# Two elementwise products moved to GpSimd, and the LayerNorm centring moved into PSUM

## The chip, the cores and the metric

The kernel runs on the 8 cores of one Trainium2 chip. Every core does the same program on one of 8 sequences, and nothing passes between cores. The metric is device time in microseconds (us) of the slowest core. The kernel before takes 775.81 us, the median of 3 runs (775.62 to 777.02).

## The reference

Per sequence, x is [2048, 1024]. A LayerNorm of x feeds two branches: a linear attention in chunks of 128 tokens with 16 heads of 64 and a decay per head, and a dense layer g with a SiLU.

```python
q, k, v = silu(x @ Wq), silu(x @ Wk), silu(x @ Wv)
def step(kv, (qi, ki, vi)):                  # per head, chunk of 128 tokens
    scores = (qi @ ki.T) * mask
    o = scores @ vi + lam_q[:, None] * (qi @ kv)
    kv = lam_c * kv + (ki * lam_k[:, None]).T @ vi
    return kv, o
o = (o - mean(o)) * rsqrt(var(o) + EPS) * gamma + beta    # over all 1024 features
gate = sigmoid(x @ Wg1 @ Wg2)
y = x0 + ((o * gate) @ Wo) * silu(x @ (W + lilora).T + b)
```

## The kernel before, in words

The script lists the operations of each engine in program order. A helper (`_emit`) turns the tiles that an operation reads and writes into semaphore waits. An engine does its own list strictly in order, so an instruction that waits holds back all that is listed behind it. A `Buf` stands for a tile or a part of one: `bPB[i]` for PSUM bank i (128 partitions of 512 f32), `bQH[0..1]` and `bKV[0..1]` for the two halves of QH and KVBD.

Five stages follow one another: LayerNorm of x, with q and k; v; the attention loop over 16 chunks (lines 592 to 706); the weights of the second branch, the gate and g; and a last stage of 16 token tiles.

The attention loop, for chunk c. TensorE computes the scores of 16 heads into banks 1 to 4 (L599, L605) and transposes K (L626, bank 0). VectorE multiplies the scores by the mask (L613, L619, twice each, into SAB), K by its decay (L631, KTM) and Q by its decay (L638, QH). Then come two halves w = 0, 1 of four head pairs: TensorE does V times scores (L649), adds the product of the carried state KVBD and QH (L662, not in chunk 0), both into banks 6 and 7, and the new state term (L669, bank 5). VectorE scales the old state half (L675) and adds bank 5 to it (L696, L701). ScalarE copies banks 6 and 7 over VO (L685, L691), the tile that L649 and L669 have read, so it waits for L669. The transposed output O thus takes the place of V. L675 of the second half is listed behind the additions of the first half and has to wait for them, since both write the same `bKV` half.

The last stage is ordered A(0), B(0), then A(tc), S(tc-1), B(tc) for tc = 1 to 15, then S(15). `p4c_A` computes the mean: eight matmuls against a column of ones (L881), a copy with 1/E (L886, MROW), an f32 matmul that spreads the row over 128 partitions (L889); VectorE subtracts it from O (L892, CC), ScalarE squares CC (L898). `p4c_B` sums the squares (L909), takes the root (L914, VROW), spreads it (L918), inverts it (L921, RBI), and does two operations on each of eight 128-column pieces of CC: times gamma and RBI (L926), plus beta and times the gate (L932). `p4c_S` multiplies piece by piece of CC with the weights, two matmuls of 512 columns for each (L946), into banks 4 and 5 for even tiles and 6 and 7 for odd ones; VectorE multiplies by G (L953) and a DMA on GpSimd's queue adds the tile to y in HBM (L958). CC has two copies, for even and odd tiles.

GpSimd has otherwise casts of small weights and one large copy of x to y, issued ahead of the attention loop (L588).

Of the kernel before, what the change touches and what calls it, by code (L numbers as in the profile page):

```python
# [8 lines left out]
AF = mybir.ActivationFunctionType  # L9
ALU = mybir.AluOpType  # L10

T = 2048
E = 1024
# [169 lines left out]
def build(debug_taps=(), stage=4):  # L183
# [82 lines left out]
    VO = mk("VO", [128, 16384], BF16, offset=off["VO"])  # L266
# [325 lines left out]
    for c in range(NCH):  # L592
# [32 lines left out]
        for f in range(8):  # L625
# [9 lines left out]
        qsrc = A(QT, 0, c * 128, [[2048, 8], [1, 128]])  # L635
        qdst = A(QH, 0, csl * 1024, [[128, 8], [1, 128]])
        lsrc = A(LAMQB, 0, 0, [[128, 8], [1, 128]])
        p.dve(lambda e, qsrc=qsrc, qdst=qdst, lsrc=lsrc: e.tensor_tensor(  # L638
            out=qdst, in0=qsrc, in1=lsrc, op=ALU.mult),
            reads=[bQT[pp][c // 4] for pp in range(8)] + [bLAMQ],  # L640
            writes=[bQH[csl]])
# [1 line left out]
        for w in range(2):  # L643
            sa, sb = 1 + 2 * w, 2 + 2 * w
            for i in range(4):
                pp = w * 4 + i
                ob = 6 + i // 2
                ocol = (i % 2) * 256
                p.pe(lambda e, pp=pp, c=c, ob=ob, ocol=ocol, w=w, i=i: e.matmul(  # L649
                    PB[ob][:, ocol:ocol + 256],  # L650
                    VO[:, c * 1024 + pp * 128:c * 1024 + (pp + 1) * 128],
                    A(SAB, 0, w * 1024 + i * 256, [[1, 256]]),
                    start=((i % 2) == 0), stop=(c == 0 and (i % 2) == 1)),
                    reads=[bVO[c][w], bSAB[w]], writes=[bPB[ob]])
            if c > 0:
                for i in range(4):
                    pp = w * 4 + i
                    ob = 6 + i // 2
                    ocol = (i % 2) * 256
                    rhs = bass.AP(QH, csl * 1024 + pp * 128,  # L660
                                  [[2048, 128], [0, 2], [1, 128]])
                    p.pe(lambda e, pp=pp, ob=ob, ocol=ocol, rhs=rhs, csl=csl, i=i: e.matmul(  # L662
                        PB[ob][:, ocol:ocol + 256],
                        KVBD[:, csl * 1024 + pp * 128:csl * 1024 + (pp + 1) * 128],
                        rhs, start=False, stop=((i % 2) == 1)),
                        reads=[bKV[csl], bQH[csl]], writes=[bPB[ob]])
            for i in range(4):
                pp = w * 4 + i
                p.pe(lambda e, pp=pp, c=c, csl=csl, i=i: e.matmul(  # L669
                    PB[5][:, i * 128:(i + 1) * 128],  # L670
                    KTM[:, csl * 1024 + pp * 128:csl * 1024 + (pp + 1) * 128],
                    VO[:, c * 1024 + pp * 128:c * 1024 + (pp + 1) * 128],
                    start=(i == 0), stop=(i == 3)),
                    reads=[bKTM[csl], bVO[c][w]], writes=[bPB[5]])
            p.dve(lambda e, csl=csl, nsl=nsl, w=w: e.tensor_tensor(  # L675
                out=KVBD[:, nsl * 1024 + w * 512:nsl * 1024 + (w + 1) * 512],
                in0=KVBD[:, csl * 1024 + w * 512:csl * 1024 + (w + 1) * 512],
                in1=LAMCB[:, w * 512:(w + 1) * 512], op=ALU.mult),
                reads=[bKV[csl], bLAMC], writes=[bKV[nsl]])
            for bb_ in range(2):  # L680
                ob = 6 + bb_
                dstA = A(VO, 0, c * 1024 + (w * 4 + bb_ * 2) * 128,
                         [[128, 2], [1, 128]], rowcount=64)
                srcA = A(PB[ob], 0, 0, [[256, 2], [1, 128]], rowcount=64)
                p.act(lambda e, d=dstA, s=srcA: e.activation(  # L685
                    out=d, in_=s, func=AF.Copy),
                    reads=[bPB[ob]], writes=[bVO[c][w]])
                dstB = A(VO, 64, c * 1024 + (w * 4 + bb_ * 2) * 128,
                         [[128, 2], [1, 128]])
                srcB = A(PB[ob], 64, 128, [[256, 2], [1, 128]])  # L690
                p.act(lambda e, d=dstB, s=srcB: e.activation(  # L691
                    out=d, in_=s, func=AF.Copy),
                    reads=[bPB[ob]], writes=[bVO[c][w]])
            oA = A(KVBD, 0, nsl * 1024 + w * 512, [[128, 4], [1, 64]], rowcount=64)
            iA = A(PB[5], 0, 0, [[128, 4], [1, 64]], rowcount=64)
            p.dve(lambda e, oA=oA, iA=iA: e.tensor_tensor(  # L696
                out=oA, in0=oA, in1=iA, op=ALU.add),
                reads=[bPB[5], bKV[nsl]], writes=[bKV[nsl]])
            oB = A(KVBD, 64, nsl * 1024 + w * 512 + 64, [[128, 4], [1, 64]])
            iB = A(PB[5], 64, 64, [[128, 4], [1, 64]])  # L700
            p.dve(lambda e, oB=oB, iB=iB: e.tensor_tensor(  # L701
                out=oB, in0=oB, in1=iB, op=ALU.add),
                reads=[bPB[5], bKV[nsl]], writes=[bKV[nsl]])
# [170 lines left out]
    def p4c_A(tc):  # L874
        par = tc % 2
        sb_st = [0, 2][par]
        sb_b = [1, 3][par]
        CCt, C2t = CCs[par], C2s[par]
        bCCt, bC2t = bCCs[par], bC2s[par]
        for pp in range(8):  # L880
            p.pe(lambda e, tc=tc, pp=pp, sb_st=sb_st: e.matmul(  # L881
                PB[sb_st][0:1, 0:128], ONESB[:, 0:1],
                VO[:, tc * 1024 + pp * 128:tc * 1024 + (pp + 1) * 128],
                start=(pp == 0), stop=(pp == 7)),
                reads=[bONESB, bVO[tc][pp // 4]], writes=[bPB[sb_st]])
        p.act(lambda e, sb_st=sb_st: e.activation(  # L886
            out=MROW[:], in_=PB[sb_st][0:1, 0:128], func=AF.Copy, scale=1.0 / E),
            reads=[bPB[sb_st]], writes=[bROW])
        p.pe(lambda e, sb_b=sb_b: e.matmul(  # L889
            PB[sb_b][:, 0:128], ONESF[:], MROW[:], start=True, stop=True),  # L890
            reads=[bONESF, bROW], writes=[bPB[sb_b]])
        p.dve(lambda e, tc=tc, CCt=CCt, sb_b=sb_b: e.tensor_tensor(  # L892
            out=A(CCt, 0, 0, [[128, 8], [1, 128]]),
            in0=A(VO, 0, tc * 1024, [[128, 8], [1, 128]]),
            in1=A(PB[sb_b], 0, 0, [[0, 8], [1, 128]]),
            op=ALU.subtract),
            reads=bVO[tc] + [bPB[sb_b]], writes=[bCCt] + bCCP[par])
        p.act(lambda e, CCt=CCt, C2t=C2t: e.activation(  # L898
            out=C2t[:], in_=CCt[:], func=AF.Square),
            reads=[bCCt] + bCCP[par], writes=[bC2t])  # L900

    def p4c_B(tc):
        par = tc % 2
        sb_st = [0, 2][par]
        sb_b = [1, 3][par]
        CCt, C2t = CCs[par], C2s[par]
        bCCt, bC2t = bCCs[par], bC2s[par]
        for pp in range(8):
            p.pe(lambda e, pp=pp, C2t=C2t, sb_st=sb_st: e.matmul(  # L909
                PB[sb_st][0:1, 128:256], ONESB[:, 0:1],  # L910
                C2t[:, pp * 128:(pp + 1) * 128],
                start=(pp == 0), stop=(pp == 7)),
                reads=[bONESB, bC2t], writes=[bPB[sb_st]])
        p.act(lambda e, sb_st=sb_st: e.activation(  # L914
            out=VROW[:], in_=PB[sb_st][0:1, 128:256],
            func=AF.Sqrt, scale=1.0 / E, bias=EPS),
            reads=[bPB[sb_st], bEPS], writes=[bROW])
        p.pe(lambda e, sb_b=sb_b: e.matmul(  # L918
            PB[sb_b][:, 128:256], ONESF[:], VROW[:], start=True, stop=True),
            reads=[bONESF, bROW], writes=[bPB[sb_b]])  # L920
        p.dve(lambda e, sb_b=sb_b: e.reciprocal(  # L921
            out=RBI[:], in_=PB[sb_b][:, 128:256]),
            reads=[bPB[sb_b]], writes=[bB128])
        for pp in range(8):
            bP = bCCP[par][pp]
            p.dve(lambda e, CCt=CCt, pp=pp: e.scalar_tensor_tensor(  # L926
                out=CCt[:, pp * 128:(pp + 1) * 128],
                in0=CCt[:, pp * 128:(pp + 1) * 128],
                scalar=GAMB[:, pp * 128:pp * 128 + 1],
                in1=RBI[:], op0=ALU.mult, op1=ALU.mult),  # L930
                reads=[bP, bB128, bLAMC], writes=[bP])
            p.dve(lambda e, tc=tc, CCt=CCt, pp=pp: e.scalar_tensor_tensor(  # L932
                out=CCt[:, pp * 128:(pp + 1) * 128],
                in0=CCt[:, pp * 128:(pp + 1) * 128],
                scalar=BETB[:, pp * 128:pp * 128 + 1],
                in1=GATE[:, pp * 2048 + tc * 128:pp * 2048 + (tc + 1) * 128],
                op0=ALU.add, op1=ALU.mult),
                reads=[bP, bBETB, bGATE[pp][tc // 4]], writes=[bP])
# [85 lines left out]
```

How the kernel before makes its waits and increments, by code:

```python
                def _run(eng):  # L119
                    for fn, waits, sem, step in self.ops[stream]:
                        for (sn, sv) in waits:
                            eng.wait_ge(self.sems[sn][0], sv)
                        if fn is not None:
                            ins = fn(eng)
                            if step:
                                ins.then_inc(self.sems[sem][0], step)
```

## Time and profile before

| | |
|---|---|
| median of 3 runs | 775.81 us |
| the profiled execution, its own time | 774.9 us |
| its span on the slowest core (core 5) | 773.3 us |
| spans of the 8 cores | 766.5 to 773.3 us |
| TensorE matmul busy | 522.2 us, 68% |
| VectorE busy | 320.6 us, 41% |
| ScalarE busy | 226.8 us, 29% |
| GpSimd busy | 19.5 us, 3% |

A busy share is an average over stages that have different limits, so the stage and its chain of waits have to be read, not the share. In the profile PE is TensorE, DVE is VectorE, ACT is ScalarE, POOL is GpSimd. PEclk is TensorE's granted clock: 1.0 is 2.4 GHz and 0.5 is 1.2 GHz, and a value between is a stretch with both. Bars of matmuls are modelled and overlap; starts are the safer thing to compare.

### The profile page before, as it was taken

How to read it: one execution, taken by the hardware profiler on the slowest of the kernel's cores; microseconds unless marked ns; L12 is line 12 of the kernel's file. 1: busy time of each engine (PE TensorE's matmuls, PEld its weight loads, DVE VectorE, ACT ScalarE, POOL GpSimd, SP SyncE). 2: the span in 40 equal slices, each digit the busy share in tenths (PEclk: the TensorE clock that was granted, in tenths of full speed). 3: DMA queues.
4: the chain of work that ended last, by engine and by line, in shares of the span. 5: the costliest groups of instructions: out<-in, count | busy, mean ns of one | idle time of the engine just before them, and what ended most of it. 6: DMA issues, size and time to landing. Idle time of an engine off the chain costs nothing.

```text
span 773.3 us, 8400 instructions; the slowest of 8 cores (766.5 to 773.3 us)
## 1 busy us (share of the span) xinstructions
PE 522.2 (68%) x2678; PEld 248.2 (32%) x2678; DVE 320.6 (41%) x675; ACT 226.8 (29%) x425; POOL 19.5 (3%) x28
## 2 busy tenths in 40 slices
PE   0118273999999971566556565799995776777673
PEld 0003131444444430344334343124442232323221
DVE  1350605110120004665566654610005777777784
ACT  1134443566333320223222232373332011111110
POOL 0000000000000000000000001000000000000000
PEclk9999595999999995555655666559997778677877
DMA  8671302000159983000000001150000332233233
GB/s 247 213 256 34 112 24 83 0 1 1 65 167 181 174 182 125 0 1 1 1 0 2 1 1 38 55 163 1 1 0 1 55 55 41 42 56 54 32 51 56
DMA packets 14049, 49.73 MB, mean 64 GB/s; under 512 B 3728, under 2 KB 3729, under 8 KB 13878
## 3 DMA queue, kind: packets, MB, share of 16 engines
q0 software_dynamic: 2448, 16.78, 13.0%
q1 hardware_dynamic: 9254, 24.02, 9.6%
q10 hardware_dynamic: 2304, 8.39, 3.7%
q8 instruction: 23, 0.38, 0.2%
q14 instruction: 20, 0.16, 0.1%
HBM read 40.79 MB, written 16.78 MB: 74 GB/s over the span
## 4 chain that ended last, share of the span: by engine, by line
PE 39%; DVE 24%; issue 10%; ACT 9%; DMA 7%; another core or an unknown queue 7%; DVEq 1%; SPq 1%; POOL 0%; ACTq 0%; POOLq 0%
PE pb L436 15%; PE pb L830 7%; PE pb L662 4%; DVE SAB L613 3%; DMA LANDB<-wq 2%; DVE CC L932 2%; DVE CCo L932 2%; DVE CC L926 2%; DVE CCo L926 2%; PE pb L817 2%; DVE RBI L921 2%; PE pb L669 2%; DMA LUPF<-lup 2%; ACT XNTM L460 2%
## 5 line engine op out<-in xcount | busy, mean ns | idle before, releaser
L436 PE MATMUL pb<-XNT,WS 128*128 128x512 bf16 x512 | 119.1, 396 | 16.0 <-ACT XNT L495 16.0
L436 PEld LDWEIGHTS pb<-XNT,WS 128*128 128x128 bf16 x512 | 51.4, 101 | 81.3 <-issue 27.3
L649 PE MATMUL pb<-SAB,VO 128*128 128x256 bf16 x128 | 31.6, 367 | 57.2 <-DVE SAB L619 34.1
L402 DVE CAST WS<-LAND 128x1024 bf16<-128x1024 f32 x20 | 13.8, 692 | 120.2 <-DMA LAND<-w 63.2
L685 ACT ACTIVATE VO<-pb 64x256 bf16<-64x256 f32 x64 | 24.2, 378 | 133.5 <-PE pb L669 130.5
L489 PE MATMUL pb<-IDB,XNTM 128*128 128x128 bf16 x128 | 13.4, 268 | 74.0 <-DVE XNTM L478 49.7
L830 PE MATMUL pb<-WS,XNT 128*128 128x512 bf16 x256 | 60.2, 390 | 0.0
L538 PE MATMUL pb<-WS,XNT 128*128 128x512 bf16 x256 | 55.6, 379 | 0.9 <-DVE WS L402 0.9
L946 PE MATMUL pb<-WS,CCo 128*128 128x512 bf16 x128 | 46.1, 529 | 5.6 <-DVE CCo L932 5.0
L946 PE MATMUL pb<-WS,CC 128*128 128x512 bf16 x128 | 46.4, 530 | 4.2 <-DVE CC L932 3.5
L662 PE MATMUL pb<-QH,KVBD 128*128 128x256 bf16 x120 | 30.7, 410 | 27.0 <-DVE QH L638 27.0
L463 DVE TENSOR_SCALAR SUMS<-SUMS 128x1 f32<-128x1 f32 x16 | 2.5, 154 | 87.3 <-ACT XNTM L460 87.3
L696 DVE TENSOR_TENSOR KVBD<-KVBD,pb 64x256 bf16<-64x256 bf16 x32 | 13.2, 413 | 59.0 <-PE pb L669 56.4
L830 PEld LDWEIGHTS pb<-WS,XNT 128*128 128x128 bf16 x256 | 25.6, 100 | 32.2 <-issue 3.6
L892 DVE TENSOR_TENSOR CC<-VO,pb 128x1024 bf16<-128x1024 bf16 x8 | 9.7, 1215 | 61.9 <-PE pb L889 61.9
L489 PEld LDWEIGHTS pb<-IDB,XNTM 128*128 128x128 bf16 x128 | 10.5, 119 | 77.3 <-issue 75.9
L538 PEld LDWEIGHTS pb<-WS,XNT 128*128 128x128 bf16 x256 | 25.0, 98 | 31.3 <-issue 1.3
L649 PEld LDWEIGHTS pb<-SAB,VO 128*128 128x128 bf16 x128 | 10.4, 108 | 72.7 <-issue 71.5
L842 ACT ACTIVATE G<-pb 128x512 bf16<-128x512 f32 x32 | 19.1, 598 | 39.2 <-PE pb L837 37.7
L545 ACT ACTIVATE VO<-pb 128x512 bf16<-128x512 f32 x32 | 19.1, 598 | 37.2 <-PE pb L538 37.2
L442 ACT ACTIVATE QT<-pb 128x512 bf16<-128x512 f32 x32 | 19.1, 598 | 32.3 <-PE pb L436 28.9
L921 DVE RECIPROCAL RBI<-pb 128x128 f32<-128x128 f32 x16 | 15.3, 958 | 29.9 <-PE pb L918 29.9
(100 smaller groups left out, 745.2 us busy)
## 6 DMA issues: line engine op xcount, KB each, us to landing
y<-SGT POOLq DMA_DIRECT2D x16, 512.0 KB, 5.3
XV<-x ACTq DMA_DIRECT2D x12, 512.0 KB, 13.4
XTS<-x ACTq DMA_DIRECT2D x4, 512.0 KB, 8.0
LAND<-wq SPq DMA_DIRECT2D x4, 512.0 KB, 5.7
LANDB<-wq SPq DMA_DIRECT2D x4, 512.0 KB, 6.1
LAND<-wk SPq DMA_DIRECT2D x4, 512.0 KB, 3.8
LANDB<-wk SPq DMA_DIRECT2D x4, 512.0 KB, 3.8
LAND<-wv SPq DMA_DIRECT2D x4, 512.0 KB, 3.4
```

The source lines that it names most:

```text
L436: p.pe(lambda e, k=k, oc=oc, t4=t4, bank=bank, wten=wten: e.matmul(PB[bank][:], wten[:, k * 1024 + oc * 128:k * 1024 + (oc + 1) * 128], XN ...
L489: p.pe(lambda e, f=f, xn=xn, bank=bank: e.matmul(pbh(bank)[:, f * 128:(f + 1) * 128], xn[:, f * 128:(f + 1) * 128], IDB[:], start=(f == 0) ...
L538: p.pe(lambda e, tc=tc, h2=h2, k=k, bank=bank: e.matmul(PB[bank][:], XNT[:, k * 2048 + tc * 128:k * 2048 + (tc + 1) * 128], WS0[:, k * 102 ...
L613: p.dve(lambda e, sa=sa, w=w: e.tensor_tensor(out=A(SAB, 0, w * 1024, [[256, 4], [1, 128]]), in0=A(PB[sa], 0, 0, [[128, 4], [1, 128]]), in ...
L649: p.pe(lambda e, pp=pp, c=c, ob=ob, ocol=ocol, w=w, i=i: e.matmul(PB[ob][:, ocol:ocol + 256], VO[:, c * 1024 + pp * 128:c * 1024 + (pp + 1 ...
L662: p.pe(lambda e, pp=pp, ob=ob, ocol=ocol, rhs=rhs, csl=csl, i=i: e.matmul(PB[ob][:, ocol:ocol + 256], KVBD[:, csl * 1024 + pp * 128:csl * ...
L685: p.act(lambda e, d=dstA, s=srcA: e.activation(out=d, in_=s, func=AF.Copy), reads=[bPB[ob]], writes=[bVO[c][w]])
L830: p.pe(lambda e, tc=tc, k=k, h=h, b0=b0: e.matmul(PB[b0 + h][:], XNT[:, k * 2048 + tc * 128:k * 2048 + (tc + 1) * 128], WS0[:, k * 1024 + ...
L921: p.dve(lambda e, sb_b=sb_b: e.reciprocal(out=RBI[:], in_=PB[sb_b][:, 128:256]), reads=[bPB[sb_b]], writes=[bB128])
L926: p.dve(lambda e, CCt=CCt, pp=pp: e.scalar_tensor_tensor(out=CCt[:, pp * 128:(pp + 1) * 128], in0=CCt[:, pp * 128:(pp + 1) * 128], scalar= ...
L932: p.dve(lambda e, tc=tc, CCt=CCt, pp=pp: e.scalar_tensor_tensor(out=CCt[:, pp * 128:(pp + 1) * 128], in0=CCt[:, pp * 128:(pp + 1) * 128], ...
L946: p.pe(lambda e, ec=ec, h=h, sb0=sb0, CCt=CCt: e.matmul(PB[sb0 + h][:], CCt[:, ec * 128:(ec + 1) * 128], WS1[:, ec * 1024 + h * 512:ec * 1 ...
```

## The change

Two products of the attention loop are issued on GpSimd in place of VectorE: Q times its decay (QH), and the scaling of the old state (KVBD). Their operands and places in the program order stay.

In the last stage, the subtraction of the mean is done by TensorE's accumulation in PSUM. The mean row is taken with its sign turned; eight matmuls with an identity copy O into the two banks that S of the same tile uses later, and two f32 matmuls of 512 columns add the negative mean. ScalarE squares from these banks, and the first of the two operations on each piece reads PSUM in place of CC. The matmul that spread the mean (L889), and the subtraction on VectorE (L892) are gone.

```diff
-        p.dve(lambda e, qsrc=qsrc, qdst=qdst, lsrc=lsrc: e.tensor_tensor(
+        p.pool(lambda e, qsrc=qsrc, qdst=qdst, lsrc=lsrc: e.tensor_tensor(
             out=qdst, in0=qsrc, in1=lsrc, op=ALU.mult),
...
-            p.dve(lambda e, csl=csl, nsl=nsl, w=w: e.tensor_tensor(
+            p.pool(lambda e, csl=csl, nsl=nsl, w=w: e.tensor_tensor(
                 out=KVBD[:, nsl * 1024 + w * 512:nsl * 1024 + (w + 1) * 512],
...
-            out=MROW[:], in_=PB[sb_st][0:1, 0:128], func=AF.Copy, scale=1.0 / E),
+            out=MROW[:], in_=PB[sb_st][0:1, 0:128], func=AF.Copy, scale=-1.0 / E),
             reads=[bPB[sb_st]], writes=[bROW])
-        p.pe(lambda e, sb_b=sb_b: e.matmul(
-            PB[sb_b][:, 0:128], ONESF[:], MROW[:], start=True, stop=True),
-            reads=[bONESF, bROW], writes=[bPB[sb_b]])
-        p.dve(lambda e, tc=tc, CCt=CCt, sb_b=sb_b: e.tensor_tensor(
-            out=A(CCt, 0, 0, [[128, 8], [1, 128]]),
-            in0=A(VO, 0, tc * 1024, [[128, 8], [1, 128]]),
-            in1=A(PB[sb_b], 0, 0, [[0, 8], [1, 128]]),
-            op=ALU.subtract),
-            reads=bVO[tc] + [bPB[sb_b]], writes=[bCCt] + bCCP[par])
-        p.act(lambda e, CCt=CCt, C2t=C2t: e.activation(
-            out=C2t[:], in_=CCt[:], func=AF.Square),
-            reads=[bCCt] + bCCP[par], writes=[bC2t])
+        sb0 = 4 + par * 2
+        for pp in range(8):
+            bank = sb0 + pp // 4
+            p.pe(lambda e, tc=tc, pp=pp, bank=bank: e.matmul(
+                PB[bank][:, (pp % 4) * 128:(pp % 4 + 1) * 128], IDB[:],
+                VO[:, tc * 1024 + pp * 128:tc * 1024 + (pp + 1) * 128],
+                start=(pp % 4 == 0), stop=False),
+                reads=[bIDB, bVO[tc][pp // 4]], writes=[bPB[bank]])
+        for h in range(2):
+            p.pe(lambda e, h=h, sb0=sb0: e.matmul(
+                PB[sb0 + h][:], ONESF[:],
+                A(MROW, 0, 0, [[0, 4], [1, 128]]),
+                start=False, stop=True),
+                reads=[bONESF, bROW], writes=[bPB[sb0 + h]])
+        for h in range(2):
+            p.act(lambda e, h=h, sb0=sb0, C2t=C2t: e.activation(
+                out=C2t[:, h * 512:(h + 1) * 512], in_=PB[sb0 + h][:],
+                func=AF.Square),
+                reads=[bPB[sb0 + h]], writes=[bC2t])
...
                 out=CCt[:, pp * 128:(pp + 1) * 128],
-                in0=CCt[:, pp * 128:(pp + 1) * 128],
+                in0=PB[sb0 + pp // 4][:, (pp % 4) * 128:(pp % 4 + 1) * 128],
                 scalar=GAMB[:, pp * 128:pp * 128 + 1],
                 in1=RBI[:], op0=ALU.mult, op1=ALU.mult),
-                reads=[bP, bB128, bLAMC], writes=[bP])
+                reads=[bP, bB128, bLAMC, bPB[sb0 + pp // 4]], writes=[bP])
```

## Rows read from the trace of the kernel before

**Rows 1.** The page, part 4: shares of the chain that ended last.

```profile
PE 39%; DVE 24%; issue 10%; ACT 9%; DMA 7%; another core or an unknown queue 7%; DVEq 1%; SPq 1%; POOL 0%; ACTq 0%; POOLq 0%
```

**Rows 2.** Windows by stage: length, busy us per engine, granted clock, DMA share, GB/s.

```profile
303.00:473.00 170.00, 102.42 (x768) 66.40 (x768) 101.44 (x193) 48.54 (x128) 0.43 (x1) 0.58 0.01 2
580.00:767.00 187.00, 128.80 (x568) 53.66 (x568) 134.77 (x320) 27.19 (x50) 13.61 (x16) 0.77 0.27 43
```

**Rows 3.** Timeline of one attention chunk: start, length, engine, line, operation, [idle before].

```profile
386.79 0.69 DVE L613 TENSOR_TENSOR SAB<-pb,MASKT 128x512 bf16<-128x512 f32 x1
...
389.59 0.68 DVE L631 TENSOR_TENSOR KTM<-pb,LAMKB 128x1024 bf16<-128x1024 bf16 x1
390.18 0.68 DVE L638 TENSOR_TENSOR QH<-QT,LAMQB 128x1024 bf16<-128x1024 bf16 x1
...
391.01 1.01 PE L662 MATMUL pb<-QH,KVBD 128*128 128x256 bf16 x4 [1.99 <-DVE QH L638]
391.82 0.63 PE L669 MATMUL pb<-VO,KTM 128*128 128x128 bf16 x4
392.55 0.38 ACT L685 ACTIVATE VO<-pb 64x256 bf16<-64x256 f32 x1 [5.02 <-PE pb L669]
...
393.14 0.42 DVE L701 TENSOR_TENSOR KVBD<-KVBD,pb 64x256 bf16<-64x256 bf16 x1
...
396.52 0.41 DVE L696 TENSOR_TENSOR KVBD<-KVBD,pb 64x256 bf16<-64x256 bf16 x1 [2.43 <-PE pb L669]
...
397.50 0.69 DVE L613 TENSOR_TENSOR SAB<-pb,MASKT 128x512 bf16<-128x512 f32 x1
```

**Rows 4.** Timeline of chunk 0, which has no L662.

```profile
306.69 0.59 PE L669 MATMUL pb<-VO,KTM 128*128 128x128 bf16 x4 [0.98 <-DVE KTM L631]
...
307.38 0.38 ACT L685 ACTIVATE VO<-pb 64x256 bf16<-64x256 f32 x1 [22.40 <-PE pb L669]
```

**Rows 5.** Timeline of GpSimd alone, ahead of the attention loop.

```profile
229.28 0.61 POOL L525 CAST WG1B<-WGL 128x512 bf16<-128x512 f32 x1 [228.59 <-DMA WGL<-wg]
236.04 1.03 POOL L529 CAST WG2B<-WGL 64x1024 bf16<-64x1024 f32 x1 [6.15 <-DMA WGL<-wg]
```

**Rows 6.** Timeline of one tile of the last stage, reciprocal to reciprocal.

```profile
666.70 0.96 DVE L921 RECIPROCAL RBI<-pb 128x128 f32<-128x128 f32 x1 [1.53 <-PE pb L918]
...
672.86 0.34 DVE L926 SCALAR_TENSOR_TENSOR CCo<-CCo,GAMB,RBI 128x128 bf16<-128x128 bf16 x1
...
673.58 1.22 DVE L892 TENSOR_TENSOR CC<-VO,pb 128x1024 bf16<-128x1024 bf16 x1
...
674.88 1.06 ACT L898 ACTIVATE CC2e<-CC 128x1024 bf16<-128x1024 bf16 x1 [6.92 <-DVE CC L892]
676.08 0.61 PE L909 MATMUL pb<-CC2e,ONESB 128*1 128x128 bf16 x8 [1.55 <-ACT CC2e L898]
...
677.93 0.96 DVE L921 RECIPROCAL RBI<-pb 128x128 f32<-128x128 f32 x1 [1.74 <-PE pb L918]
```

**Rows 7.** Chain of waits: start, length, what; runs of matmuls at either clock.

```profile
395.07 0.85 PE pb L662 x4
...
521.09 3.45 PE pb L830 x16
```

**Rows 8.** Windows over the first 5.6 us of L946, three of sixteen tiles.

```profile
590.10:595.70 5.60, 5.60 (x16) 1.84 (x16) 4.87 (x15) 0.00 (x0) 0.00 (x0) 0.60 0.01 3
...
691.40:697.00 5.60, 5.60 (x14) 1.85 (x15) 4.87 (x15) 0.00 (x0) 0.00 (x0) 0.50 0.21 42
...
758.70:764.30 5.60, 5.45 (x16) 1.57 (x16) 4.17 (x15) 0.00 (x0) 0.00 (x0) 0.72 0.25 49
```

**Rows 9.** Timeline: an f32 spread, and the last tile's reciprocal and product.

```profile
668.10 0.76 PE L889 MATMUL pb<-MROW,ONESF 1*128 1x128 f32 x2 [0.56 <-ACT MROW L886]
...
756.62 0.96 DVE L921 RECIPROCAL RBI<-pb 128x128 f32<-128x128 f32 x1 [1.73 <-PE pb L918]
...
764.28 1.49 DVE L953 TENSOR_TENSOR SGT<-pb,G 128x512 f32<-128x512 f32 x2 [0.70 <-PE pb L946]
```

More of the change, by code:

```diff
@@ L923, in p4c_B @@
             reads=[bPB[sb_b]], writes=[bB128])
+        sb0 = 4 + par * 2
         for pp in range(8):
             bP = bCCP[par][pp]
-            p.dve(lambda e, CCt=CCt, pp=pp: e.scalar_tensor_tensor(
+            p.dve(lambda e, CCt=CCt, pp=pp, sb0=sb0: e.scalar_tensor_tensor(
                 out=CCt[:, pp * 128:(pp + 1) * 128],
-                in0=CCt[:, pp * 128:(pp + 1) * 128],
+                in0=PB[sb0 + pp // 4][:, (pp % 4) * 128:(pp % 4 + 1) * 128],
                 scalar=GAMB[:, pp * 128:pp * 128 + 1],
                 in1=RBI[:], op0=ALU.mult, op1=ALU.mult),
-                reads=[bP, bB128, bLAMC], writes=[bP])
+                reads=[bP, bB128, bLAMC, bPB[sb0 + pp // 4]], writes=[bP])
             p.dve(lambda e, tc=tc, CCt=CCt, pp=pp: e.scalar_tensor_tensor(
```

## The prediction

> **What bounds the kernel now.** I read the page's chain first: TensorE and VectorE hold most of it and GpSimd nothing [rows 1], so no busy share tells what an edit is worth. The windows by stage come next: the change touches two stages, the attention loop (170 us) and the last stage (187 us) [rows 2], and in both VectorE and TensorE are each busy 60 to 72% of the time. Two engines that both idle a third of a stage mean a ring of waits, so I read one turn of either ring in the timeline.
>
> Attention, one chunk [rows 3]: 10.71 us from L613 to the next L613 (386.79 to 397.50). VectorE does the four mask products, KTM until 390.27, QH until 390.86. L662 starts at 391.01, listed as waiting for QH; L669 follows at 391.82; ScalarE's copies wait for L669, since they write over the tile that it reads; and all of the second half hangs on those copies. QH is thus on the ring, the scaling of the state is not.
>
> Last stage, one tile [rows 6]: 11.23 us from reciprocal to reciprocal. After the reciprocal come 16 piece operations on VectorE, the eighth L926 ending at 673.20; then the subtraction (1.22 us), the square (1.06 us), L909, root, spread, and 677.93. The 16 matmuls L946 are not in this ring: they run piece by piece beside VectorE's 16 operations and end while it subtracts.
>
> **Attention, the moved products.** Without QH, L662 has nothing of VectorE to wait for. L649 needs the first two mask products, done at about 388.3; L649 and L662 are four matmuls of 256 columns each, 0.85 us per four at the lower clock [rows 7], so L662 is through by 390.1. L669 then waits for KTM: 390.27 plus the 0.15 us that lay between QH's end and L662, so 390.42 in place of 391.82. That is 1.40 us sooner, and everything behind it (copies, second half, next scores) moves with it. Chunk 0 is the pattern: there L669 waits for KTM already, and the first copy follows its start by 0.69 us, as in the loop by 0.73 [rows 3, 4]. It gains nothing; 15 chunks gain 1.40 each: **-21.0 us**.
>
> This stands only if GpSimd keeps pace. Its list per chunk is QH, first scaling, second scaling. The second waits for L701 of the first half, which would end 5.4 us into the chunk (393.56 less 386.79, less 1.4). Its result is due at 8.3 (396.52 less 386.79 less 1.4), the next QH, queued behind it, at 11.8 (the next chunk begins at 9.3, its L662 2.5 later), the next first scaling at about 13.7. With d for a scaling (512 columns) and q for QH (1024): d at most 2.9, d + q at most 6.4, 2d + q at most 8.3 us. GpSimd's two casts took 0.61 us for 512 and 1.03 for 1024 columns [rows 5]; they read one tile and the products two. The lower bound is the cast: 2d + q = 2.3. There is no row for an upper one. I double the casts for the second input: 4.5, with 3.8 us spare. Behind these products GpSimd has only the L744 cast and nothing that is due early; ahead of them is the issue of the large copy, over 50 us earlier. So the two edits cost nothing else.
>
> The Trainium skill (GPSIMD Engine Reference, section 3.1) speaks against such moves: about 2.6 cycles an element for a product of two tiles at 1.2 GHz, the VectorE about twice as fast. By that estimate q is 2.2 and d 1.1 us, 4.4 together, and the sum would stay as it is. No row of this trace has such a product on GpSimd.
>
> **Last stage, what goes.** Subtraction and square leave the ring: A(tc+1) no longer passes through VectorE, so mean, identity matmuls, f32 matmuls and squares can all run while VectorE is at its 16 operations. The work added there is 8 matmuls of 128 columns (as many columns as four of 256: 0.85 us at the lower clock [rows 7]) and two f32 matmuls of 512. A 128-column f32 spread is two passes, 0.76 us at the lower clock [rows 9]; two of 512 columns cost eight times that at most, 6.1 us, and at the bf16 rate four passes of 0.43, 1.7 us, at least. I take 3.5, between the two. The mean row is there about 1.5 us after the reciprocal, so this ends about 5 us after it, and two squares of about 0.6 each end by 6.3. The first of the ring's needs comes at 6.65 (below), so it is hidden; at the upper bound it ends at 7.6 and would push by about 1 us a tile.
>
> **Last stage, what is late next.** The O minus mean now lies in the very banks into which S of the same tile accumulates, and `_emit` counts a bank as one tile. The second matmul of S (first piece, second half) writes the bank that holds pieces 4 to 7, so it must wait until the eighth L926 has read it. That is 6.50 us after the reciprocal [rows 6]; with 0.15 for the handover, 6.65. Fifteen matmuls of 512 columns then run with nothing of VectorE beside them, and behind them on TensorE stand L909 and L918, on which the next reciprocal waits. L909 to reciprocal takes 1.85 us [rows 6]. So one turn becomes 6.65 + b + 1.85, b being the 15 matmuls.
>
> At granted 1.0, 16 such matmuls take 3.45 us [rows 7], so b = 3.24. At 0.50, four of 256 take 0.85, so 512 columns take 0.425 and b = 6.4. The clock in L946's first 5.6 us was 0.60 in the first tile, 0.72 in the last, 0.50 in the lowest of the sixteen, 0.63 in their mean [rows 8]; in each it began low, after TensorE had done little between the tiles. The new turn has that pause again, straight ahead of the 15, so I use 0.63: b = 3.24 / 0.63 = 5.1. The turn is 13.6 us against 11.23: 2.37 more, in 15 turns **+35.6 us**. The last tile has the same wait: its L953 started 7.66 us after its reciprocal [rows 9] and would start at 6.65 + 5.1 = 11.75: **+4.1 us**. The first tile trades 1.22 + 1.06 us of subtraction and square for matmuls and two squares of about the same sum: 0.
>
> The rule behind this in the Trainium skill (TensorE: Matmul & The Clock Gate, Part 1) is that TensorE's default is the throttled clock and that activity releases it. By it the identity and f32 matmuls might keep the clock up; by the same rule the pause behind them takes it away. The trace agrees with the second, L946 having begun at the low clock.
>
> L926 reads PSUM in place of SBUF. L696 reads PSUM too and takes 0.41 for 256 columns [rows 3], so 128 columns can add no more than 0.07 to the 0.34 of L926: 0 to 0.5 us a tile, 0 to 8 in all. I take 0, since a longer operation of this kind has the whole start-up in it already.
>
> **Sum**, against the profiled execution's own 774.9 us: 774.9 - 21.0 + 39.7 = 793.6. The median of the runs is 0.9 above that execution, so I say **794 us**, 2.3% slower.
>
> **Rivals.**
> 1. *The clock stays up through the 15 matmuls.* For it: the added identity and f32 matmuls fill a part of the pause. Against: none of sixteen tiles kept 1.0 [rows 8]. Then b = 3.24, the turn 11.74: +7.7, the last tile +2.2, together 774.9 - 21.0 + 9.9 = **764 us**, faster. It decides where 16b - 42 falls under 21 (15 turns of b - 2.73, and b - 1.0 at the end): b under 3.9 us, a mean granted clock over 0.82.
> 2. *The clock stays low through them.* The lowest of rows 8 speaks for it. b = 6.4: +55.1 and +5.4, so 774.9 - 21.0 + 60.5 = **814 us**.
> 3. *GpSimd is too slow or contends with VectorE.* If 2d + q exceeds 8.3, the chunk grows by the excess. At four times the casts it is 9.0: 0.7 of the 1.4 us is lost, 804 us; at 9.7 the whole gain is lost, **815 us**. The Trainium skill (SBUF — State Buffer, Who interferes with whom) has a VectorE instruction with two SBUF inputs blocked by a GpSimd one that reads SBUF. All of VectorE's operations left in this loop have one input from PSUM [rows 3], so by that page too this would not occur.
> 4. *The wait doesn't come as I say*: S's second matmul isn't held by the eighth L926, and S runs beside VectorE as now, to end 7.7 us after the reciprocal (L953's start [rows 9]). L909 would follow there and not at 9.38 [rows 6]: 1.7 us less a turn, 25 in all, 774.9 - 21.0 - 25 = **729 us**. Against it stand the lists of reads and writes: one buffer a bank.
>
> **How the numbers follow.** Forecast with b between 4.4 and 5.8 (782 to 805): 0.58. Rival 1 and what lies up to the break-even: 0.15. Rival 2: 0.14. Rival 3: 0.10. Rival 4: 0.01. The rest, 0.02, is an answer within 0.2%, which is about what the measurement can tell from no change. Faster is 0.16, same 0.02, slower 0.82. The range runs from rival 1 to a little over rivals 2 and 3, with half of the PSUM bound: 763 to 818 us; the likeliest case alone spans 782 to 805.
>
> **What would show it.** In attention: chunks of 9.3 us, L669 of the first half waiting for KTM, no wait on QH. The GpSimd products at about 2.1 and 1.2 us. In the last stage: L946 listed as waiting for L926, one matmul ahead of the wait and 15 behind it in 5.1 us, the idle time of VectorE's reciprocal or L953 behind L946 grown to about 4 us a tile, and turns of 13.6 us. The prediction is wrong if the 15 matmuls run at granted 1.0, if the turn is bounded by the f32 matmuls (L909 waiting for squares), or if the attention chunk doesn't shrink.

## The result and the profile after

The changed kernel takes 791.97 us (median of 9 runs) against 775.10 us (10 runs): a ratio of 1.021, 95% interval 1.0193 to 1.0228: slower, clear of no change, with 2% inside the interval. Forecast were 794 us, 2.3% slower.

In some executions the cores of one die show a lower granted clock and take longer; the ratios leave these out, and as the profiled execution of the changed kernel is one of them, the readings below are from core 2 of its other die (span 789.9 us), set against core 5 of before (773.3 us).

From the page after, which shows core 6, the slowest: engine, busy us, share of the span, instructions; and the shares of the chain that ended last.

```profile
PE 564.8 (70%) x2838; PEld 264.4 (33%) x2838; DVE 284.3 (35%) x611; ACT 228.9 (28%) x441; POOL 89.4 (11%) x76
...
PE 49%; DVE 21%; issue 8%; another core or an unknown queue 6%; ACT 6%; DMA 6%; DVEq 1%; SPq 1%; POOL 0%; ACTq 0%; POOLq 0%
```

VectorE lost 36 us of work, GpSimd took on 70, and TensorE's share of the chain rose from 39% [rows 1] to 49% (48% on core 2). GpSimd's share of it stayed at 0%.

One attention chunk after, timeline of core 2, columns as in rows 3:

```profile
385.64 0.69 DVE L613 TENSOR_TENSOR SAB<-pb,MASKT 128x512 bf16<-128x512 f32 x1
...
388.08 1.06 PE L662 MATMUL pb<-QH,KVBD 128*128 128x256 bf16 x4
388.44 0.68 DVE L631 TENSOR_TENSOR KTM<-pb,LAMKB 128x1024 bf16<-128x1024 bf16 x1
389.27 0.59 PE L669 MATMUL pb<-VO,KTM 128*128 128x128 bf16 x4
389.95 0.38 ACT L685 ACTIVATE VO<-pb 64x256 bf16<-64x256 f32 x1 [3.57 <-PE pb L669]
...
390.55 0.42 DVE L701 TENSOR_TENSOR KVBD<-KVBD,pb 64x256 bf16<-64x256 bf16 x1
391.12 1.15 POOL L675 TENSOR_TENSOR KVBD<-KVBD,LAMCB 128x512 bf16<-128x512 bf16 x1 [4.09 <-DVE KVBD L701]
392.22 2.12 POOL L638 TENSOR_TENSOR QH<-QT,LAMQB 128x1024 bf16<-128x1024 bf16 x1
393.92 0.41 DVE L696 TENSOR_TENSOR KVBD<-KVBD,pb 64x256 bf16<-64x256 bf16 x1 [2.95 <-PE pb L669]
394.89 0.69 DVE L613 TENSOR_TENSOR SAB<-pb,MASKT 128x512 bf16<-128x512 f32 x1
```

It answers rows 3: 9.25 us from L613 to L613 in place of 10.71. L662 has no wait; L669 starts 3.63 us into the chunk (389.27), right behind KTM, where it was 5.03. GpSimd's scaling is through at 392.27 and is wanted at 393.92.

One turn of the last stage after, reciprocal to reciprocal, timeline of core 2:

```profile
659.53 0.96 DVE L928 RECIPROCAL RBI<-pb 128x128 f32<-128x128 f32 x1
...
660.52 1.95 PE L898 MATMUL pb<-MROW,ONESF 1*128 1x512 f32 x4
...
662.62 0.60 ACT L904 ACTIVATE CC2e<-pb 128x512 bf16<-128x512 f32 x1 [0.32 <-PE pb L898]
...
663.24 0.38 PE L954 MATMUL pb<-WS,CCo 128*128 128x512 bf16 x1 [0.77 <-DVE CCo L934]
...
665.61 0.34 DVE L934 SCALAR_TENSOR_TENSOR CCo<-pb,GAMB,RBI 128x128 bf16<-128x128 f32 x1
...
666.11 3.15 PE L954 MATMUL pb<-WS,CCo 128*128 128x512 bf16 x7 [2.49 <-DVE CCo L934]
...
671.51 0.61 PE L916 MATMUL pb<-CC2e,ONESB 128*1 128x128 bf16 x8
671.61 1.49 DVE L961 TENSOR_TENSOR SGT<-pb,G 128x512 f32<-128x512 f32 x2 [5.19 <-PE pb L954]
...
673.18 0.96 DVE L928 RECIPROCAL RBI<-pb 128x128 f32<-128x128 f32 x1
```

It answers rows 6: 13.65 us in place of 11.23. One matmul of S slips in at 663.24, itself held until the fourth L934 had read the first of the two banks, and the second waits 2.49 us for L934, the eighth of which ends at 665.95. The other 15 run from 666.11 to 671.51, with VectorE idle for 5.19 us. The squares had been ready since 663.2. Windows over those 15 matmuls, columns as in rows 2; the first tile, one of the middle, the last:

```profile
568.90:574.20 5.30, 4.72 (x12) 1.73 (x13) 0.79 (x3) 0.00 (x0) 0.00 (x0) 0.50 0.00 0
...
666.10:671.40 5.30, 5.08 (x14) 1.87 (x15) 0.31 (x1) 0.00 (x0) 0.00 (x0) 0.60 0.00 0
...
775.40:780.70 5.30, 5.30 (x15) 1.83 (x15) 0.28 (x1) 0.00 (x0) 0.00 (x0) 0.61 0.02 3
```

And the windows of the turn shown: from its reciprocal to the end of the wait, then the first and the last microsecond of the 15 matmuls.

```profile
659.50:666.10 6.60, 3.34 (x21) 1.50 (x19) 5.64 (x17) 1.46 (x3) 0.87 (x1) 0.80 0.51 82
...
666.10:667.10 1.00, 0.99 (x3) 0.41 (x4) 0.31 (x1) 0.00 (x0) 0.00 (x0) 0.50 0.00 0
670.50:671.50 1.00, 1.00 (x5) 0.29 (x3) 0.00 (x0) 0.00 (x0) 0.00 (x0) 1.00 0.00 0
```

On this core the granted clock is only ever 1.0 or 0.5, so a mean of 0.80 over 6.6 us is 2.6 us at 0.5: the clock fell at 663.5, when most of the wait was still to come, and it rose at 670.3, inside the 15 matmuls.

The last tile, timeline of core 2, answers rows 9: 12.05 us from reciprocal to L961, where it was 7.66.

```profile
768.80 0.96 DVE L928 RECIPROCAL RBI<-pb 128x128 f32<-128x128 f32 x1
...
780.85 1.49 DVE L961 TENSOR_TENSOR SGT<-pb,G 128x512 f32<-128x512 f32 x2 [5.17 <-PE pb L954]
```

### The profile page after: what moved, and what is told of

It reads as the page before. It is cut to its first block, busy times and chain, and to the rows that moved or that the text cites. A ratio compares the mean times of both kernels' runs of the same rounds, so it can differ in the third digit from the quotient of the medians.

```text
span 805.5 us, 8728 instructions; the slowest of 8 cores (783.4 to 805.5 us)
## 1 busy us (share of the span) xinstructions
PE 564.8 (70%) x2838; PEld 264.4 (33%) x2838; DVE 284.3 (35%) x611; ACT 228.9 (28%) x441; POOL 89.4 (11%) x76
## 3 DMA queue, kind: packets, MB, share of 16 engines
q0 software_dynamic: 2448, 16.78, 12.6%
## 4 chain that ended last, share of the span: by engine, by line
PE 49%; DVE 21%; issue 8%; another core or an unknown queue 6%; ACT 6%; DMA 6%; DVEq 1%; SPq 1%; POOL 0%; ACTq 0%; POOLq 0%
PE pb L436 17%; PE pb L954 11%; PE pb L830 7%; DMA LANDB<-wq 3%; DVE CCo L940 2%; DVE CC L940 2%; DVE CCo L934 2%; DVE CC L934 2%; DVE SGT L961 2%; PE pb L662 2%; DVE SAB L613 2%; PE pb L649 2%; PE pb L538 2%; PE pb L817 2%
## 5 line engine op out<-in xcount | busy, mean ns | idle before, releaser
L436 PE MATMUL pb<-XNT,WS 128*128 128x512 bf16 x512 | 136.3, 438 | 16.3 <-ACT XNT L495 16.3
L436 PEld LDWEIGHTS pb<-XNT,WS 128*128 128x128 bf16 x512 | 55.4, 109 | 94.3 <-issue 85.8
L489 PE MATMUL pb<-IDB,XNTM 128*128 128x128 bf16 x128 | 14.3, 281 | 73.4 <-DVE XNTM L478 48.4
L402 DVE CAST WS<-LAND 128x1024 bf16<-128x1024 f32 x20 | 16.4, 820 | 128.1 <-DMA LAND<-w 55.9
L675 POOL TENSOR_TENSOR KVBD<-KVBD,LAMCB 128x512 bf16<-128x512 bf16 x32 | 36.8, 1150 | 139.5 <-DVE KVBD L701 66.6
L961 DVE TENSOR_TENSOR SGT<-pb,G 128x512 f32<-128x512 f32 x32 | 22.1, 692 | 83.0 <-PE pb L954 81.4
L966 POOL DMA_DIRECT2D y<-SGT x16 | 13.8, 864 | 312.0 <-DVE SGT L961 312.0
L921 ACT ACTIVATE VROW<-pb 1x128 f32<-1x128 f32 x16 | 4.3, 267 | 132.1 <-PE pb L916 132.1
L954 PEld LDWEIGHTS pb<-WS,CCo 128*128 128x128 bf16 x128 | 15.7, 127 | 61.8 <-issue 58.9
L954 PEld LDWEIGHTS pb<-WS,CC 128*128 128x128 bf16 x128 | 15.5, 126 | 58.0 <-issue 54.9
## 6 DMA issues: line engine op xcount, KB each, us to landing
XV<-x ACTq DMA_DIRECT2D x12, 512.0 KB, 12.6
```

The source lines that it names most:

```text
L402: p.dve(lambda e, k=k, dten=dten, land=land: e.tensor_copy(out=dten[:, k * 1024:(k + 1) * 1024], in_=land[:]), reads=[lb], writes=[bufs[k]])
L436: p.pe(lambda e, k=k, oc=oc, t4=t4, bank=bank, wten=wten: e.matmul(PB[bank][:], wten[:, k * 1024 + oc * 128:k * 1024 + (oc + 1) * 128], XN ...
L489: p.pe(lambda e, f=f, xn=xn, bank=bank: e.matmul(pbh(bank)[:, f * 128:(f + 1) * 128], xn[:, f * 128:(f + 1) * 128], IDB[:], start=(f == 0) ...
L675: p.pool(lambda e, csl=csl, nsl=nsl, w=w: e.tensor_tensor(out=KVBD[:, nsl * 1024 + w * 512:nsl * 1024 + (w + 1) * 512], in0=KVBD[:, csl * ...
L954: p.pe(lambda e, ec=ec, h=h, sb0=sb0, CCt=CCt: e.matmul(PB[sb0 + h][:], CCt[:, ec * 128:(ec + 1) * 128], WS1[:, ec * 1024 + h * 512:ec * 1 ...
L961: p.dve(lambda e, tc=tc, h=h, sb0=sb0, sgt=sgt: e.tensor_tensor(out=sgt[:, h * 512:(h + 1) * 512], in0=PB[sb0 + h][:], in1=G[:, tc * 1024 ...
```

## The experiments

In all of them the turns named are from the profiled execution of that kernel, on its slowest core if no other is named, reciprocal to reciprocal. A ratio is to the kernel before, run beside it.

**Either part alone.** The kernel before with only the two `p.dve` turned to `p.pool`:

```diff
-        p.dve(lambda e, qsrc=qsrc, qdst=qdst, lsrc=lsrc: e.tensor_tensor(
+        p.pool(lambda e, qsrc=qsrc, qdst=qdst, lsrc=lsrc: e.tensor_tensor(
...
-            p.dve(lambda e, csl=csl, nsl=nsl, w=w: e.tensor_tensor(
+            p.pool(lambda e, csl=csl, nsl=nsl, w=w: e.tensor_tensor(
...
```

> The kernel before with only the two products moved to GpSimd; the last stage is the old one. Theory (both parts add up as predicted): a chunk of 9.3 us in place of 10.7, 15 of them, so 775.1 - 21.9 = 753 us, and last-stage turns of 11.23 us as before. Rival (the part of the change that slows is in the attention loop, or contention between GpSimd and VectorE eats the gain): 770 us or more.

752.79 us, ratio 0.9707 (0.9689 to 0.9725). And the kernel before with only the last stage changed, the diff of the change without these two hunks:

> The kernel before with only the last stage changed; both products stay on VectorE. Theory: turns of 13.65 us as in the changed kernel, so 775.1 + 15 x 2.4 + about 4 = 814 us. Rival (the two parts interact, the last stage is dearer only behind the shortened attention loop): well under 805 us.

816.79 us, ratio 1.0524 (1.0502 to 1.0546), its turns 13.65 us in the steady part. Against the 775.91 us of the kernel before in these runs, the change is a gain of 23 us and a loss of 41, and the two add up: 775.1 - 23.1 + 40.9 is 792.9, against 791.97 measured.

**QH alone.** Only the first of the two hunks above.

> Only QH is moved to GpSimd, the scaling of the state stays on VectorE. Theory (QH alone is on the ring of the chunk): the same chunk of 9.3 us and 753 us, within 2 us of the kernel with both products moved. Rival (the scaling's 0.4 us behind KTM on VectorE is on the ring once QH is gone): 0.3 to 0.4 us more a chunk for one or both halves, 758 to 765 us.

752.44 us, ratio 0.9700 (0.9682 to 0.9717), no different from both moved. The whole gain is QH's; moving the scaling of the state was worth nothing.

**Is GpSimd's cover real?** QH computed three times. This kernel has the old last stage, so its base is the kernel with the two moves, 752.79 us, and not the changed one as the expectation has it; what was expected on that base is 17 us more, 770.

```diff
+        for _rep in range(3):
             p.pool(lambda e, qsrc=qsrc, qdst=qdst, lsrc=lsrc: e.tensor_tensor(
...
```

> The changed kernel with QH computed three times over on GpSimd (same result). It tests the cover of the moved products: now the scaling of the second half (1.15 us), three QH (2.12 each) and then L662, L669, L696 and L701 of the next chunk (2.55 us from L662's start to L701's end) form a ring. Theory (dependencies as read): 1.15 + 6.36 + 2.55 and handovers of about 0.3, a chunk of 10.4 us in place of 9.25, 15 times 1.15 us more than the changed kernel: 809 us. Rival (only GpSimd's sum counts, two scalings and three QH are 8.66 us, under 9.25): no change, 792 us.

772.26 us, 19.5 more than that base. Its timeline on core 5 (the added line moves the numbers of those below it by one):

```profile
401.99 1.15 POOL L676 TENSOR_TENSOR KVBD<-KVBD,LAMCB 128x512 bf16<-128x512 bf16 x1 [1.47 <-DVE KVBD L702]
...
403.10 6.64 POOL L639 TENSOR_TENSOR QH<-QT,LAMQB 128x1024 bf16<-128x1024 bf16 x3
...
409.89 0.83 PE L663 MATMUL pb<-QH,KVBD 128*128 128x256 bf16 x4 [1.88 <-POOL QH L639]
```

TensorE waits for QH again, and most chunks are 10.60 us. GpSimd's sum (two scalings and three QH, 8.9 us) is under the old 9.25 us chunk, so the sum doesn't bound it: the ring through the second scaling does, as expected. The change itself stays clear of that by two QH less.

**The bank wait taken away.** S gets banks 2 and 3 for itself; the statistics of even and odd tiles share banks 0 and 1.

```diff
-        sb_st = [0, 2][par]
-        sb_b = [1, 3][par]
+        sb_st = 0
+        sb_b = 1
...
-        sb0 = 4 + par * 2
+        sb0 = 2
```

(The first two in `p4c_A` and `p4c_B`, the third in `p4c_S` alone.)

> The changed kernel, but S accumulates into banks 2 and 3 and not into those that hold O minus mean; the statistics of even and odd tiles share banks 0 and 1 to make room. Theory (the wait of S's second matmul for the eighth L934 is what costs): the matmuls run piece by piece beside VectorE again, turns of 9.5 to 11 us in place of 13.65, 740 to 755 us. Rival (the added identity and f32 matmuls cost it, since TensorE does its list in order, much of it at the lower clock): turns stay at 13 us or more and the time at 785 us or more.

732.19 us, ratio 0.9438 (0.9407 to 0.9469), 60 us less than the changed kernel and a better one than before. Two turns on core 0:

```profile
640.85 0.96 DVE L928 RECIPROCAL RBI<-pb 128x128 f32<-128x128 f32 x1
...
644.47 6.21 PE L954 MATMUL pb<-WS,CC 128*128 128x512 bf16 x15
...
652.28 0.96 DVE L928 RECIPROCAL RBI<-pb 128x128 f32<-128x128 f32 x1
...
655.16 4.75 PE L954 MATMUL pb<-WS,CCo 128*128 128x512 bf16 x16
...
661.51 0.96 DVE L928 RECIPROCAL RBI<-pb 128x128 f32<-128x128 f32 x1
```

S now starts 2.9 to 3.6 us after the reciprocal and runs beside VectorE. On this core most turns are of two lengths, 11.43 us (S in 6.2 us) and 9.23 us (S in 4.8), mean 10.24; on other cores many are 9.8 us, with means down to 9.77. The identity and f32 matmuls are all still there, so the added work was not what cost. Nor was it the statistics' banks: the kernels with useless matmuls below share them in the same way and keep the wait. Against the kernel with the two moves alone (752.79 us, run beside it) this one is 20.6 us faster: the centring in PSUM is itself a gain, 1.3 us a tile, once S doesn't have to wait for its banks.

**Fewer matmuls left for the end.** The banks stay shared, S's loops are turned:

```diff
-        for ec in range(8):
-            for h in range(2):
+        for h in range(2):
+            for ec in range(8):
```

> The changed kernel with one loop order turned: S does its eight matmuls of the first bank, then the eight of the second. The bank wait stays, but only the second bank's eight matmuls are behind it. Theory (15 matmuls behind the wait cost 5.1 to 5.4 us a turn): eight of them cost 1.7 to 3.4 us, turns of 10.5 to 12.1 us in place of 13.65, 750 to 770 us. Rival (the turn is set by the clock's changes, one turn per full change down and up, and not by the count behind the wait): turns stay at 13.65 us, 790 us.

756.27 us, ratio 0.9780 (0.9750 to 0.9811). Turns of 10.7 to 12.8 us, mean 11.7, but not quite for the reason given. A turn on core 5:

```profile
642.69 0.96 DVE L928 RECIPROCAL RBI<-pb 128x128 f32<-128x128 f32 x1 [0.39 <-PE pb L925]
...
646.40 5.42 PE L954 MATMUL pb<-WS,CCo 128*128 128x512 bf16 x16 [0.77 <-DVE CCo L934]
...
649.23 0.35 DVE L940 SCALAR_TENSOR_TENSOR CCo<-CCo,BETB,GATE 128x128 bf16<-128x128 bf16 x1
```

The only bank wait left to see is the first, for the fourth L934: S starts 3.7 us after the reciprocal and runs beside VectorE. Its eighth matmul needs the last piece, which the eighth L940 finishes at 6.9 us; the second bank had been read by then, so the eight matmuls behind it are late by their place in the list and not by the bank. Eight matmuls left for the end cost some 2 us a turn less than fifteen, and the turn isn't bound to 13.65 us by the clock, as the rival had it.

**The wait made early.** VectorE's operations in another order, all L934 and then all L940:

```diff
                 reads=[bP, bB128, bLAMC, bPB[sb0 + pp // 4]], writes=[bP])
+        for pp in range(8):
+            bP = bCCP[par][pp]
             p.dve(lambda e, tc=tc, CCt=CCt, pp=pp: e.scalar_tensor_tensor(
...
```

> The changed kernel with VectorE's piece operations in another order: all eight L934, then all eight L940. The banks are read out about 3 us after the reciprocal in place of 6.5, and no operation stands right behind the one whose result it reads (0.45 us from start to start in the pairs, 0.27 between pairs). Theory: the 16 matmuls start when the f32 matmuls are through, 3 to 5 us after the reciprocal, and take 3.5 to 6.8: turns of 9.2 to 12 us, 730 to 765 us. Rival (the added TensorE work sets the turn): 785 us or more.

740.01 us, ratio 0.9560 (0.9535 to 0.9586), turns mostly of 10.24 to 10.53 us. On core 1 the eight L934 and the eight L940 (here L942) take 2.2 us each, where the pairs took 5.8 together:

```profile
677.68 0.96 DVE L928 RECIPROCAL RBI<-pb 128x128 f32<-128x128 f32 x1
...
678.74 2.16 DVE L934 SCALAR_TENSOR_TENSOR CCo<-pb,GAMB,RBI 128x128 bf16<-128x128 f32 x8
...
680.82 2.18 DVE L942 SCALAR_TENSOR_TENSOR CCo<-CCo,BETB,GATE 128x128 bf16<-128x128 bf16 x8
681.30 5.01 PE L956 MATMUL pb<-WS,CCo 128*128 128x512 bf16 x16 [0.68 <-DVE CCo L942]
```

The last read of the shared bank is over at 680.90, and all 16 matmuls run on from 681.30 behind the first L942, beside the other seven. Two things changed here, the early end of the wait and VectorE's 1.6 us less for its operations, and this kernel alone doesn't part them.

**The low clock of the 15 matmuls.** The pause ahead of them filled with matmuls whose result nothing reads (`PB[2]`, with the statistics in banks 0 and 1), 12 of them and 6:

```diff
+                if ec == 0 and h == 0:
+                    for _k in range(12):
+                        p.pe(lambda e, tc=tc: e.matmul(
+                            PB[2][:], VO[:, tc * 1024:tc * 1024 + 128],
+                            VO[:, tc * 1024:tc * 1024 + 512],
+                            start=True, stop=True),
...
```

> The changed kernel with 12 useless matmuls of 512 columns (bf16, into bank 2, which nothing reads; the statistics share banks 0 and 1) put behind S's first matmul, where TensorE otherwise pauses for the eighth L934. Theory (the pause ahead is what lowers the clock, and the low clock makes the 15 matmuls 5.4 us instead of 3.2): granted clock 1.0 in them, turns of 11.8 to 12.4 us, 765 to 775 us though TensorE does more. Rival (the clock drops for another reason): the twelve run at 0.5 too, 5.1 us from about 3.8 after the reciprocal, and the turn becomes 16 us or more, 825 us or more.

785.33 us, ratio 1.0158 (1.0120 to 1.0196): between the two, the forecast of time missed. A turn on core 2, L961 here being the filler:

```profile
674.65 5.04 PE L961 MATMUL pb<-VO 128*128 128x512 bf16 x12
679.52 3.40 PE L954 MATMUL pb<-WS,CC 128*128 128x512 bf16 x15
682.85 0.61 PE L916 MATMUL pb<-CC2o,ONESB 128*1 128x128 bf16 x8
```

The 15 matmuls do run at 1.0 (0.93 at the least, in the shorter turns) and take 3.3 to 3.6 us, as expected. But the twelve ran mostly at the lower clock and took 4.9 us, ending 2.4 us after the point where the wait would have ended. The low stretch moved from the 15 to the filler. Turns of 14.03 us like this one alternate with turns of 13.20, in which the twelve take 4.2; the mean is 13.8.

> As the kernel with 12 useless matmuls in the pause, with 6: they fit into the pause at either clock (1.3 us at 1.0, 2.6 at 0.5). Theory (the clock over the 15 matmuls is set by what TensorE did before them): with half of the pause filled their clock lies between, b of 3.3 to 5.0 us and turns of 11.8 to 13.3 us, 764 to 787 us. Rival (only a filled pause helps): turns of 13.65 as in the changed kernel, 790 us.

773.59 us, ratio 0.9974 (0.9955 to 0.9993): turns of 11.6 to 14.4 us, mean 12.6. The wait ends where it did, 6.6 us after the reciprocal, and the 15 matmuls take from 3.33 us (granted 1.0) to 5.9 us (0.56). Useless work made the changed kernel 18 us faster, some 1.2 us a turn. Together the two show that the clock over the 15 matmuls hangs on what TensorE did before, and that the low clock costs 2.1 us of the turn of 13.65 (5.40 less 3.33). They also speak against the expectation's wording that the pause is what lowers the clock: in all three kernels it falls 2 to 5 us after the reciprocal, filler or not. What the filler moves is the rise: 8.2 to 8.8 us after the reciprocal with twelve, in place of 10.8; with six it comes sooner in most turns (from 6.4 us) and later in two (11.8 and 12.0), those of 14.3 and 14.4 us.

**The f32 matmuls.** The mean row in bf16, and with it the two spread matmuls:

```diff
-                PB[sb0 + h][:], ONESF[:],
+                PB[sb0 + h][:], ONESB[0:1, :],
```

> The changed kernel with the mean row in bf16, so that the two spread matmuls of 512 columns are bf16 (two passes of 0.2 to 0.4 us in place of four f32 ones, 1.95 us at granted 1.0). Theory (this work is hidden behind VectorE's operations and the turn waits for the eighth L934): no change, 790 us and turns of 13.65 us, or a little longer if TensorE, with more of a pause, is at the lower clock for all 15 matmuls (14.6 us, 806 us). Rival (the added TensorE work is on the path): at least 1 us less a turn, 775 us or less.

790.90 us, ratio 1.0201 (1.0169 to 1.0233), turns of 13.65 us: no change. The two spread matmuls take 0.59 us in place of 1.95, and the wait ends 6.58 us after the reciprocal as before. This work was hidden, as the prediction had it.

**A version from these.** S in banks 2 and 3, and VectorE's operations staggered, the first one of piece n+1 ahead of the second one of piece n; then the same with the mean row in bf16.

```diff
-        for pp in range(8):
-            bP = bCCP[par][pp]
-            p.dve(...)  # first operation of piece pp
-            p.dve(...)  # second operation of piece pp
+        for q in range(9):
+            if q < 8:
+                pp = q
+                bP = bCCP[par][pp]
+                p.dve(...)  # first operation of piece pp
+            if q > 0:
+                pp = q - 1
+                bP = bCCP[par][pp]
+                p.dve(...)  # second operation of piece pp
```

> A version put together from what was found: the changed kernel with S in banks 2 and 3, and VectorE's operations staggered (the first one of piece n+1 ahead of the second one of piece n), so that none stands right behind the one it reads. Theory: 16 operations at 0.27 us a start are 4.3 us in place of 5.8, and TensorE's list becomes the bound: turns of 8.8 to 10 us against 10.24 with the banks alone, 712 to 730 us. Rival (TensorE's list at the lower clock was the bound already): 10.2 us and 732 us.

724.60 us, ratio 0.9343 (0.9314 to 0.9371), turns of 9.79 and 8.11 us, mean 9.54.

> The version before with the mean row in bf16. Here, unlike in the changed kernel, the spread matmuls stand in front of S on an engine that is the bound: theory 1.1 to 2 us less a turn than with f32, turns of 7.8 to 9 us, 690 to 715 us. Rival (VectorE and the handovers bound the turn): within 0.3 us a turn of the f32 version.

704.83 us, ratio 0.9083 (0.9050 to 0.9116): 9% faster than the kernel before. Its turns are 7.83 us in most tiles, mean 8.36. The same edit that was worth nothing in the changed kernel is worth 20 us here: the spread now stands right in front of S, which starts 2.1 us after the reciprocal in place of 2.9. Not tried was the old last stage with VectorE's operations staggered, so nothing here says how much of the 9% needs the centring in PSUM.

## Why the prediction was right

The mechanism is the one forecast, in both parts: QH left the ring of the chunk, and S fell behind VectorE's last read of its banks. The closeness of 791.97 to 794 is in part luck, since the attention loop gained 3.7 us more than forecast and the last stage lost 2.4 us more. By its own steps, on core 2 against core 5 of before:

- *Attention, -21.0.* From the first KTM to the cast after the loop it is 166.7 us before and 142.0 after, 24.7 less. A chunk at the lower clock gained 1.46 us, near the 1.40; most of the rest comes from shorter chunks, such as the one from 379.85 to 388.44, in which the granted clock was 0.72 in the mean:

```profile
379.80:388.40 8.60, 5.22 (x46) 3.77 (x47) 4.96 (x10) 3.02 (x8) 4.38 (x3) 0.72 0.00 0
385.60:394.90 9.30, 6.88 (x51) 4.33 (x50) 4.96 (x11) 3.07 (x9) 4.38 (x3) 0.50 0.01 2
```

  Behind chunk 0, eleven of 14 chunks before took 10.71 us, at granted clocks of 0.50 to 0.68. After, eight took 9.25, at 0.50 to 0.67; three at 0.59 or 0.60 took 9.05, and three at 0.72 to 0.80 took 8.6 to 8.7. That more of the ring is TensorE's without QH, so that a faster clock shortens it, is my reading and was not tested. I had left it out.
- *GpSimd.* d was taken as 1.2 and is 1.15, q as 2.1 and is 2.12. The Trainium skill's estimate (GPSIMD Engine Reference, section 3.1) of 1.1 and 2.2 agrees with these rows too. Its ratio doesn't: the same products took VectorE 0.42 and 0.68 us, so GpSimd is 2.7 to 3.1 times slower here, not about twice.
- *The added TensorE work hidden.* Right; the four f32 passes take 1.95 us at granted 1.0, less than the 3.5 I took.
- *The bank wait, +35.6.* It ends at 6.58 us, not 6.65; b is 5.40, not 5.1; L916 to reciprocal 1.67, not 1.85. The turn is 13.65 for 13.6. The three errors cancel. The 15 turns came to 206.5 us against 168.8, +37.7, the first two being longer (14.8 and 13.9).
- *The clock behind b.* It was 0.61, near the 0.63 that I took over from the old stage, but that was a guess and its reason was off. I wrote that L946 began at the low clock in each tile; in the trace of before it began at 1.0 in four of sixteen, and the clock fell 0.1 to 0.7 us later. And the low clock isn't the work of the pause: it falls about as the wait begins, and the pause only puts off its rise.
- *Last tile, +4.1.* +4.4.
- *L926's source in PSUM, 0.* 0.34 us before and after.
- *The first tile, 0.* From its first mean matmul to its reciprocal it is 8.5 us before and 8.2 after.
- The stretch between attention and the last stage, which the change doesn't touch, came out 2.4 us shorter in this execution, and the wait for weights ahead of the loop 1.8 longer.
- The rivals: a b near 3.24 (3.33) was seen only with the pause filled. GpSimd contending with VectorE was not seen: L696 took 0.41 us whether it ran beside a GpSimd product or not. But all of VectorE's operations that ran beside one have an input in PSUM, as that rival says of them, and KTM never did run beside one; with QH alone moved, the scaling that stays on VectorE has two SBUF inputs, and it too never ran beside QH. So contention of that kind stays untested.

## What to carry to other kernels

Before a result is left in PSUM to spare an engine a pass, ask which instruction writes that bank next and how far behind it the last reader is: here the pass and the square behind it had taken 2.3 us of a turn, and its bank held back 15 matmuls for 2.5 us and took them out of VectorE's shadow. With two other banks for S the same change was a gain. An elementwise product can go to an engine that is about three times slower if its inputs are ready early and the ring through that engine, not its sum, has been worked out. Work that follows a pause on TensorE is to be priced at the clock that the trace shows there, and the price stays a guess as long as the new turn differs from the old.

## What was not expected

The turn after settles at 13.65 us to within 0.01, for three to seven tiles in a row, on cores of both dies, in the changed kernel, with the last stage alone, and with the bf16 row, though the work in it differs by 1.4 us of TensorE; a turn of 13.9 interrupts it, and it drifts back. In each such turn the granted clock fell once, 4.0 us after the reciprocal, and rose once, 10.8 us after it, so that the 15 matmuls met the rise at the same place: the last stage and the clock keep step. Why it settles there was not tried.

A pair of VectorE operations of which the second reads the first's result costs 0.45 + 0.27 us from start to start, 0.72 in all, and 0.52 when another operation stands between. The stage has 128 of these pairs, which makes an estimate of 26 us of VectorE's time, more than the 20 us of the subtraction (1.22 us a tile). But the time gained is what counts: with the banks freed, staggering them took 732.19 to 724.60 us, 7.6 less.
